# Attention-weighted aggregation on one core: one-hots that carry alpha, made by two engines

## The reference, cut to what matters

```
msg = silu(x_src @ W_node * scale + edge_sh @ W_sh)          # per edge, 128 channels
a = silu(...); a = silu(...); a = a @ aW3 + ab3              # per edge, 8 heads
alpha = softmax(a, axis=0)                                   # over all edges, for each head
alpha_mean = alpha.mean(axis=1, keepdims=True)               # one number per edge
agg = segment_sum(msg * alpha_mean, dst, num_segments=6250)
out = layernorm(node_features + agg @ W_out)
```

## Time and profile before

| | us |
|---|---|
| median of 3 runs | 3744.99 (3740.04 to 3747.55) |
| span of the profiled execution | 3741.0 |
| aggregation loop in it, 3347.3 to 3677.7 | 330.4 |
| after it (`finish`) | 63.3 |

### The profile page before, as it was taken

One profiled execution on the slowest core, in us unless ns is written; L12 is line 12 of the kernel. 1 busy time (PEld: TensorE's weight loads), 2 busy tenths in 40 slices (PEclk: granted clock), 3 DMA queues, 4 the chain that ended last, 5 costly groups with the idle time before them and its releaser, 6 DMA issues. The chain is left out here.

```text
span 3741.0 us, 80383 instructions
## 1 busy us (share of the span) xinstructions
PE 2977.1 (80%) x16644; PEld 1907.1 (51%) x16868; DVE 2959.2 (79%) x4980; ACT 2396.7 (64%) x5055; POOL 2113.4 (56%) x2168
## 2 busy tenths in 40 slices
PE   0657777777777777544999999999999999968885
PEld 0345555555555555422555555555555555547774
DVE  5689999999999999883777777777777777667776
ACT  8345555555555555453777777777777777758885
POOL 2177777777777777423666666666666666610001
PEclk9979999999999999977999999999999999989998
DMA  5655445444544444224777777777777777736673
GB/s 172 186 154 145 144 140 140 142 144 140 143 142 141 143 143 143 77 80 134 221 223 221 221 222 219 219 224 219 219 222 220 220 223 219 223 122 202 201 202 88
DMA packets 438076, 654.90 MB, mean 175 GB/s; under 512 B 87013, under 2 KB 267807, under 8 KB 438018
## 3 DMA queue, kind: packets, MB, share of 16 engines
q1 hardware_dynamic: 288962, 306.73, 28.6%
q0 software_dynamic: 98304, 268.57, 24.1%
q10 hardware_dynamic: 50752, 78.99, 5.9%
HBM read 549.87 MB, written 103.95 MB: 175 GB/s over the span
## 5 line engine op out<-in xcount | busy, mean ns | idle before, releaser
L1322 POOL DMA_INDIRECT l_G<-rows_d,l_sidx x1024 | 994.8, 972 | 581.2 <-ACT l_h L1462 296.2
L901 POOL DMA_INDIRECT l_G<-rows_d,l_sidx x1024 | 1015.5, 992 | 330.3 <-issue 304.7
L969 PE MATMUL l_accp<-l_we,l_ohe 128*128 128x256 f32 x2048 | 487.9, 381 | 0.0
L925 PE MATMUL l_A<-ident,l_G 128*128 128x128 f32 x1024 | 172.9, 293 | 381.0 <-DVE l_oht L1072 319.3
L1462 ACT ACTIVATE l_h<-l_H,l_cols 128x512 f32<-128x512 f32 x512 | 348.3, 680 | 187.6 <-PE l_H L1369 174.1
L969 PEld LDWEIGHTS l_accp<-l_we,l_ohe 128*128 128x128 f32 x2048 | 372.7, 192 | 40.5
L1592 DVE TENSOR_TENSOR l_msg<-l_G,l_ST 128x512 f32<-128x512 f32 x256 | 175.9, 687 | 273.1 <-issue 180.7
L997 ACT ACTIVATE l_qe<-l_A 128x512 f32<-128x512 f32 x256 | 153.1, 598 | 326.5 <-PE l_A L928 211.2
L925 PEld LDWEIGHTS l_A<-ident,l_G 128*128 128x128 f32 x1024 | 111.2, 144 | 483.2 <-DVE l_oht L1072 237.9
L1743 PE MATMUL ag_accp<-ag_msg,ag_pick 128*128 128x128 f32 x2048 | 289.4, 288 | 72.4 <-ACT ag_msg L1727 33.4
L1092 DVE TENSOR_TENSOR_SCAN l_qe<-l_lo,l_qe 128x512 f32<-128x512 bf16 x256 | 325.9, 1273 | 0.3
(11 more groups left out here) (205 smaller groups left out, 6655.1 us busy)
## 6 DMA issues: line engine op xcount, KB each, us to landing
l_raw<-in_ea_dram SPq DMA_DIRECT2D x1024, 64.0 KB
msg_d<-l_msg ACTq DMA_DIRECT2D x256, 256.0 KB
ag_msg<-msg_d SPq DMA_DIRECT2D x256, 256.0 KB, 2.9
l_G<-rows_d,l_sidx POOLq DMA_INDIRECT x2048
l_lo<-mark_d SPq DMA_DIRECT2D x256, 128.0 KB, 2.9
l_lo<-code_d SPq DMA_DIRECT2D x256, 128.0 KB
l_fd<-dst_d SPq DMA_DIRECT2D x256, 96.0 KB, 3.4
l_pd<-dst_d SPq DMA_DIRECT2D x256, 96.0 KB
```

The source lines that it names most:

```text
L901: nc.gpsimd.indirect_dma_start(out=G[:, s, j, :], out_offset=None, in_=rows_d[0][:, :], in_offset=bass.IndirectOffsetOnAxis(ap=sidx[:, hal ...
L925: nc.tensor.matmul(av[:, j, :], G[:, s, j, 0:C], ident[:, :], is_transpose=True, start=(j == 0), stop=False, skip_group_check=True)
L969: last = nc.tensor.matmul(accp[b][:, 0:2 * C], oh_e[:, b, j, :], we_t[:, b, j, :], start=(j == 0), stop=(j == TJ - 1), skip_group_check=True)
L1322: nc.gpsimd.indirect_dma_start(out=G[:, s, j, :], out_offset=None, in_=rows_d[1][:, :], in_offset=bass.IndirectOffsetOnAxis(ap=sidx[:, hal ...
```

## The change

ACT's scaling of the messages goes, and DVE's too. Instead the one-hots carry alpha: at the edge's destination stands alpha and not 1, made by one two-operation instruction for each block ((iota == local) * alpha), with two per-partition scalars. DVE makes blocks 0 and 1 of every item, straight into `ag_pick`, and POOL blocks 2 and 3. POOL copies the columns of `local` and `alpha` for eight items at a time into `near` (two halves, each of eight items), waits for its copies, and takes the scalars from there; its program has a turn of 16 items. PE waits for the load itself, for DVE's one-hots, for POOL's one-hots and for `acc_done`.

```diff
+            BESIDE = 2
+            HERE = TJ - BESIDE
...
+                near = sb("ag_near", [P, 2, 2, U * TJ], F32, st)
...
+                near_ready = sem("ag_near_ready", st)
+                beside_ready = sem("ag_beside_ready", st)
...                     # POOL
+                        pool.wait_ge(s_alpha, 1)
+                        al = alpha[:, (HEADS - 1) % 2, :]
+
+                        def step(lap, u):
+
+                            i, v, lp = item(lap, u, 0, 2 * U)
+                            s, half = v % U, v // U
+                            if not exists(i, NI):
+                                return
+                            if after(i, R):
+                                hold(pool, pool_passed, (accp_ready, i - R + 1))
+                            if s == 0:
+                                if after(i, 2 * U):
+                                    hold(pool, pool_passed, (beside_ready, BESIDE * (i - U)))
+                                nc.gpsimd.tensor_copy(near[:, half, 0, :], local[:, bass.ds(i * TJ, U * TJ)]).then_inc(near_ready, 1)
+                                nc.gpsimd.tensor_copy(near[:, half, 1, :], al[:, bass.ds(i * TJ, U * TJ)]).then_inc(near_ready, 1)
+                                hold(pool, pool_passed, (near_ready, 4 * lp + 2 * half + 2))
+                            for j in range(TJ - BESIDE, TJ):
+                                t = s * TJ + j
+                                nc.gpsimd.tensor_scalar(pick[:, s % R, j, :], iota_row[:, :], near[:, half, 0, t:t + 1],
+                                                        near[:, half, 1, t:t + 1], ALU.is_equal,
+                                                        ALU.mult).then_inc(beside_ready, 1)
+                        run_items(pool, step, LAPS // 2, 2 * U)
...                     # ACT: its scaling loop is gone
-                                nc.scalar.activation(mine, mine, ACT.Copy,
-                                                     scale=al[:, bass.ds(i * TJ + j, 1)]).then_inc(shared, 1)
...                     # PE
-                            pe.wait_ge(shared, lp * SHARED[-1] + SHARED[s])
-                            pe.wait_ge(pick_ready, lp * PICKED[-1] + PICKED[s])
+                            pe.wait_ge(ld[s], 16 * (lp + 1))
+                            pe.wait_ge(pick_ready, HERE * (i + 1))
+                            pe.wait_ge(beside_ready, BESIDE * (i + 1))
...                     # DVE, weigh
-                            nc.vector.tensor_tensor(pick[:, b, :, :], iota_row[:, :].unsqueeze(1).to_broadcast([P, TJ, P]),
-                                                    local[:, bass.ds(i * TJ, TJ)].unsqueeze(2).to_broadcast([P, TJ, P]),
-                                                    ALU.is_equal).then_inc(pick_ready, 1)
-                            if OWN[s] == TJ:
-                                return
-                            dve.wait_ge(ld[s], 16 * (lp + 1))
-                            mine = msg_t[:, s, 0, :]
-                            nc.vector.tensor_scalar(mine, mine, al[:, bass.ds(i * TJ, 1)], None,
-                                                    ALU.mult).then_inc(pick_ready, 1)
+                            for j in range(HERE):
+                                nc.vector.tensor_scalar(pick[:, b, j, :], iota_row[:, :], local[:, bass.ds(i * TJ + j, 1)],
+                                                        al[:, bass.ds(i * TJ + j, 1)], ALU.is_equal,
+                                                        ALU.mult).then_inc(pick_ready, 1)
```

More of the change, by code:

```diff
@@ L1660, in layer1_aggregate @@
             T = NI * TJ
-            OWN = [TJ - 1 + s % 2 for s in range(U)]
-            SHARED = [sum(OWN[0:s + 1]) for s in range(U)]
-            PICKED = [sum(1 + TJ - n for n in OWN[0:s + 1]) for s in range(U)]
+            BESIDE = 2
+            HERE = TJ - BESIDE
             st = ExitStack()
@@ L1685, in layer1_aggregate @@
                 s_alpha = sem("ag_alpha_ready", st)
-                shared = sem("ag_shared", st)
+                near_ready = sem("ag_near_ready", st)
+                beside_ready = sem("ag_beside_ready", st)
                 pick_ready = sem("ag_pick_ready", st)
@@ L1715, in _ @@
                                                  accum_out=tot[:, h:h + 1]).then_inc(s_ex, 1)
[L1716 to L1722, removed]
-                                return
-                            act.wait_ge(ld[s], 16 * (lp + 1))
-                            for j in range(TJ - OWN[s], TJ):
-                                mine = msg_t[:, s, j, :]
-                                nc.scalar.activation(mine, mine, ACT.Copy,
-                                                     scale=al[:, bass.ds(i * TJ + j, 1)]).then_inc(shared, 1)
-                        run_items(act, step)
                     @block.tensor
```

## The result

The changed kernel takes 3846.05 us (median of 4 runs, 3845.01 to 3846.62) against 3743.61 (4 runs): ratio 1.0273, 95% interval 1.0258 to 1.0287. It is slower by 102 us, where 13 were forecast; the time lies outside the stated range. The profiled spans differ by the same amount, 3843.7 against 3741.0.

The account below looks back on a forecast made before the run. DVE's issue path was taken as the bound; +0.56, +0.12 and -0.20 made +0.48 us a lap, x 30 = +14.4, with -1 in constant items +13 on 3745.0: 3758 us. Range 3742 to 3800, own range 3750 to 3766.

Parts of the forecast that it names:

- What bounds the kernel before: Aggregation loop: DVE's issue path, not busy time, sets the pace, at 10.40 us a lap of eight items.
- ACT's scalings: Aggregation loop: removing ACT's 896 scalings (282.7 us busy) gains 0, at most 0.5 us.
- POOL's two one-hots: POOL in the loop: 0.35 us each, 0.85 an item with copies and waits, hidden under 1.35.
- POOL becomes the bound: Rival, loop: POOL and DVE one-hots exclude each other, 1.48 us an item, +49 us, 3794 us; chance 0.17.
- Its second form: Same rival, loop: POOL one-hots of 0.684 us without exclusion, 1.47 us an item; within the rival's chance 0.17.
- c = 0.15: DVE's issue in the loop: each second two-pointer instruction costs 0.15 us (bounds 0.05 and 0.25), +0.56 a lap.
- 0.015 for the first one's second address: DVE's first tensor_scalar of an item: its second register address adds 0.015 us, +0.12 a lap.
- The start: Before the first product: POOL's two copies and two one-hots replace ACT scalings, 0 within 0.5 us.
- The faster rival: Loop: DVE's issue runs ahead, items follow busy time and PE at 1.14 us, -38 us, 3707 us; chance 0.12.
- The fourth wait of PE: PE's sequencer: waiting on four counters, not three, costs 0; without cover 0.1 us an item.

Follow-up runs that it names:

- the written-out loop: The kernel before with its aggregation loop given constant addresses and semaphore values, nothing else changed: median 3673.5 us, ratio 0.9859.
- DVE alone: The changed kernel with POOL's one-hots after the first four items left out: 3789.4 us, ratio 1.0125.
- the written-out loop with three of them an item: The changed kernel with constant addresses, three of four one-hots on DVE, one on POOL, and an early POOL tensor_scalar: 3668.9 us, ratio 0.9806.
- POOL alone: The changed kernel with DVE's one-hots after the first four items left out, POOL's two and DVE's adds kept: 3833.4 us.
- three one-hots on DVE: The changed kernel with three one-hots of an item on DVE and one on POOL, loop in registers: 3829.2 us.
- the written-out changed kernel: The changed kernel with its aggregation loop written out with constant addresses: 3839.2 us.

## Why the prediction was wrong

*What bounds the kernel before*: right. DVE's issue path set the pace; the written-out loop (-68 us) and the scaling moved off DVE (-17 us, 18 expected) together show it. That ACT's scalings were worth nothing in the looped kernel fits: with them gone and POOL's one-hots left out the time still follows DVE's lap. No run takes them away alone, and in the written-out loop, where ACT is busy without a gap, the same account wouldn't hold.

*POOL's two one-hots, "I take 0.35 ... hidden under 1.35"*: this is the step that failed. The instruction takes 0.79 us, above even my upper bound of 0.684, so the pair with its share of copies is 1.64 an item and not 0.85. The bounds were rows of instructions without per-partition scalars; a row of another operation is no bound when the cost depends on operands that it doesn't have. (The fit between the two POOL rows also has a slip, 2884 / 1280 in place of the slope between them, 2.15 ns a column; it gives 0.41 for 0.40 and changes nothing.) The lap went from 10.40 to about 13.2, and this term sets it. Of the 93 us between the first and the last add 40 would have come from DVE's own path (below), which lies hidden behind POOL's; the other 53 are POOL's alone.

*The rival "POOL becomes the bound"*: the mechanism that happened, at 0.17. Its price of 3794 rested on two full exclusions with DVE (0.68 of the 1.48) and 0.40 of work. It was the reverse: 0.77 of work each, while DVE's company costs 10 us in all. Its second form, a slow POOL without exclusion, was the nearer one, but at 1.47 an item for the 1.65 that came, as its 0.684 was too low.

*The price of a second two-pointer instruction, c = 0.15, and 0.015 for the first one's second address*: mis-sized. Summed they gave +0.48 a lap; DVE alone has 11.75, +1.35. The register work is 93 ns for each of the two and 40 more in most items. By itself this would have made the change slower by about 40 us (367.0 from the first add to the last, 326.8 before), outside my 3750 to 3766 as well. It is hidden behind POOL in the kernel that ran.

*The start, "0 within 0.5 us"*: wrong by 9 us, 7.65 of them the wait behind the configuration change ahead of POOL's first tensor_scalar.

*The faster rival*: false. Shorter arithmetic on DVE (0.60 in place of 0.69 and 0.28) bought nothing while its addresses were formed in registers. *The fourth wait of PE* cost nothing that a run shows.

## What to carry to other kernels

Where a hardware loop's items last about a microsecond, count the sequencer's instructions and the addresses that each data instruction forms, not busy time: here one instruction of 512 columns with one register address gave an item of 1.09 us, two of 128 with two addresses each one of 1.36. Before work is moved to POOL, time that very form of instruction, with its pointers and both operations, on the chip, both alone and beside the other engine's work; and look for a change of configuration ahead of its first use. If an engine's idle time is put down to a partner, check with the timeline whether the partner had finished long before.

## What the runs showed that was not expected

- A POOL tensor_scalar of 128 float32 columns takes 0.78 us with two operations and two pointers, 0.60 with one of each; by the two widths measured, 64 and 128, an estimated 0.35 of the 0.78 is fixed and 3.3 ns go with each column.
- In the changed kernel DVE's 128-column instructions lengthen a POOL one-hot by only 0.02 us (0.77 to 0.79 from start to start). In the written-out loop with three of them an item, where DVE is never idle, it takes 0.93 on average. DVE's 512-column instruction with two inputs on chip stretches a POOL scaling that starts behind it from 0.60 to 0.93. The Trainium skill ("SBUF — State Buffer", Who interferes with whom) says that a VectorE instruction with two SBUF inputs contends with a GpSimd one that reads SBUF; the rows with 0.93 agree.
- PE's granted clock was 0.94 on average over the loop in place of 0.99 (1.00 is the level of 2.4 GHz, so a few stretches fell to the level of 1.2). From 3380 to 3650 PE is busy 193.9 of 270 us here at a clock of 0.96, but 193.8 us with POOL alone and 191.4 us with three one-hots on DVE, both at 1.00, so PE's longer idle time alone is no explanation, and the cause stays open. It isn't what made the change slow: with POOL alone the lap is still 12.90 us at 1.00, and in the written-out changed kernel 13.03 at 0.99.
